# Mixture stages: GpSimd issues its row transfers to the slots in fours, each four behind a unit of the shared expert

## The chip, the core and the metric

The kernel runs on one core of a Trainium2 chip. TensorE (PE) multiplies matrices, VectorE (DVE) and ScalarE (ACT) work elementwise, GpSimd (POOL) does small elementwise work and issues the indirect DMAs, SyncE (SP) issues the plain ones. The metric is device time in microseconds, lower is better. The engines run their own instruction streams and meet at semaphores.

## What is computed

Two layers of sequence mixing and feed-forward blocks on 4096 tokens of width 256 (float32). The change concerns the last block of each half of the second layer, `_L1_ffn_ref`, which the program calls twice (stages `moe1` and `moe2`):

```python
x = x + _L1_attn_a_ref(_layernorm(x), ...)
x = x + _L1_ffn_ref(_layernorm(x), ...)      # stage moe1
x = x + _L1_attn_b_ref(_layernorm(x), ...)
x = x + _L1_ffn_ref(_layernorm(x), ...)      # stage moe2

def _L1_ffn_ref(x, gate_w, gate_bias, w_gate, w_up, w_down, sw_gate, sw_up, sw_down):
    B, N, H = x.shape
    xf = x.reshape(-1, H)
    topk_idx, topk_w = _gate(xf, gate_w, gate_bias)        # 2 of 8 experts for each token
    g = silu(einsum('th,ehi->tei', xf, w_gate))
    u = einsum('th,ehi->tei', xf, w_up)
    experts_y = einsum('tei,eih->teh', g * u, w_down)
    masked_y = take_along_axis(experts_y, topk_idx[:, :, None], axis=1)
    y = einsum('tkh,tk->th', masked_y, topk_w).reshape(B, N, H)
    shared = silu(x @ sw_gate) * (x @ sw_up) @ sw_down     # the shared expert, every token
    return y + shared
```

## The kernel before

Tokens lie in `TILES` = 32 tiles of 128, in `G` = 8 groups of four tiles. A mixture stage (`stage_moe`) normalises the tokens, transposes them for TensorE, computes the router's scores, and on VectorE chooses two experts for each token and works out a place (slot) for each of the 8192 pairs of token and choice, so that the rows of one expert stand together in DRAM (`xd`, shown in the profile as `moe_slots_moe`).

Two pieces of work then run side by side:

- **The row transfers.** GpSimd issues 64 indirect DMAs (`TOP_K` = 2 choices times 32 tiles, L2016). Each scatters the 128 rows of a tile (256 values and the token's number, 1028 bytes a row) to their slots. Before each eight of them GpSimd copies the numbers of the tokens into the rows (L2013). Each completion counts on `sent[k]`. SyncE waits for all of them (L1968) and only then loads the slots back, tile by tile (L1965), for the routed experts.
- **The shared expert.** It runs in `UNITS` = `G * SB_` = 16 units n, two for a group (blocks b = 0, 1 of the hidden width 256). TensorE's `up(n)` (L2060) multiplies gate and up weights, four products of 128x512 that the trace shows as eight matmuls; ScalarE's `silu(n)` (L2171) waits for it; VectorE's `product(n)` (L2252) multiplies and raises `prod_ready` by one. After the second unit of group g, TensorE's `down(g)` (L2069) waits for both products and writes four tiles to PSUM; it signals `y_ready` after each two of them, and VectorE adds these to `x` (`add`, L2258). The accumulators are two pairs of banks (`hp` for even n, `trp` for odd n), so `up(n)` waits for `prod_ready` at n - 1. TensorE's order is up(0), up(1), the two count products of the router, up(2), down(0), up(3), up(4), down(1) and so on. Units 0 and 1 come before the slots are known, the others beside the row transfers.

When both are done, the **routed experts** follow in 72 tiles: TensorE transposes a loaded tile (L2107), multiplies by its expert's weights (L2113, L2126), and GpSimd scatters the result to `yd` by another indirect DMA (L2020). TensorE reaches this part after down(7), whose end is also the end of the shared expert.

Nothing in the kernel before ties the row transfers to the progress of the shared expert: GpSimd issues all 64 as fast as it can from the moment that the places of the first choice are there (`idx_ready`).

Of the kernel before, what the change touches and what calls it, by code (L numbers as in the profile page):

```python
# [23 lines left out]
TILES = T // P  # L24
# [1799 lines left out]
TOP_K = 2  # L1824
# [52 lines left out]
def stage_moe(c, name, out=None):  # L1877
# [2 lines left out]
    we, ws, wsd, wr, bias, order, count, w = (m[n] for n in ("we", "ws", "wsd", "wr", "bias", "order", "count", "w"))  # L1880
    ids, starts, xd, yd, w_loaded = m["ids"], m["starts"], m["xd"][name], m["yd"], m["loaded"]
    UNITS = G * SB_
    with Local(c, name) as s:
        st = s.sb("bn_stats", [P, TILES, 6])
        mv = s.sb("moments", [P, TILES, 2])
# [45 lines left out]
        up_filled, silu_ready, prod_ready = s.sem("up_filled"), s.sem("silu_ready"), s.sem("prod_ready")  # L1931
# [15 lines left out]
        with ExitStack() as banks:  # L1947
# [13 lines left out]
            with nc.Block() as block:  # L1961
# [25 lines left out]
                @block.gpsimd  # L1987
                def _(pool):
                    pool.memset(half[:, :], -0.5).then_inc(half_ready, 1)
                    pool.memset(eps[:, :], EPS).then_inc(half_ready, 1)  # L1990
                    pool.memset(less[:, :], -1.0).then_inc(half_ready, 1)
                    pool.wait_ge(half_ready, 3)
                    for g in range(G):
                        at = slice(g * GT, (g + 1) * GT)
                        pool.wait_ge(moments_ready, g * GT + GT)
                        pool.tensor_tensor(ve[:, at], mv[:, at, 1], eps[:, :], ALU.add).then_inc(eps_added, 1)
                        pool.tensor_tensor(minus[:, at], mv[:, at, 0], less[:, :], ALU.mult).then_inc(eps_added, 1)
                        pool.wait_ge(eps_added, 2 * g + 2)
                        pool.tensor_tensor(rstd[:, at], ve[:, at], half[:, :], ALU.pow).then_inc(rstd_ready, 1)
                        pool.wait_ge(rstd_ready, g + 1)  # L2000
                        pool.tensor_tensor(shift[:, at], minus[:, at], rstd[:, at], ALU.mult).then_inc(shift_ready, 1)
                    pool.wait_ge(m["xd_padded"], 32)
                    pool.wait_ge(xn_ready, TILES // 2)
                    pool.wait_ge(xa_ready, TILES // 2)
                    pool.wait_ge(w_loaded, 16 * MOE_LOADS)
                    for choice in range(TOP_K):
                        pool.wait_ge(idx_ready, choice + 1)
                        for t in range(TILES):
                            k = t // CHUNK
                            if t % CHUNK == 0:  # L2010
                                if choice > 0:
                                    pool.wait_ge(sent[k], 16 * CHUNK)
                                pool.tensor_copy(xr[:, t:t + CHUNK, D:ROW].bitcast(U32).rearrange("p t o -> p (t o)"),  # L2013
                                                 ids[:, choice, t:t + CHUNK]).then_inc(id_ready, 1)
                                pool.wait_ge(id_ready, choice * CHUNKS_X + k + 1)
                            pool.indirect_dma_start(xd, bass.IndirectOffsetOnAxis(ap=idx[:, choice, t:t + 1], axis=0), xr[:, t, :],  # L2016
                                                    None).then_inc(sent[t // CHUNK], 16)
                    for i in range(SLOT_TILES):
                        pool.wait_ge(yt_ready, i + 1)
                        pool.indirect_dma_start(yd, bass.IndirectOffsetOnAxis(ap=xg[:, i % XRING, D:ROW].bitcast(U32), axis=0),  # L2020
                                                yb[:, i % XRING, :], None, bounds_check=TOP_K * T - 1,
                                                oob_is_err=False).then_inc(y_sent[i % XRING], 16)

                @block.tensor
                def _(pe):
# [48 lines left out]
                    def up_and_down(n):  # L2074
                        up(n)
                        if n % 2 == 0:
                            down(n // 2 - 1)
# [3 lines left out]
                    for g in range(1, G):  # L2081
# [12 lines left out]
                      .then_inc(counted, 1)  # L2094
                    for n in range(2, UNITS):
                        up_and_down(n)
                    down(G - 1)

                    pe.wait_ge(prod_ready, UNITS)
                    pe.wait_ge(added, 2 * G)  # L2100
# [60 lines left out]
                def _(act):  # L2161
# [21 lines left out]
                    def scores(n):  # L2183
                        act.wait_ge(logits_ready, n + 1)
                        for j in range(GT):
                            last = act.activation(score[:, n * STRIPS * GT:(n + 1) * STRIPS * GT, :].rearrange("p (i j) e -> p i j e", j=GT)[:, :, j, :],
                                                  back[n][:, j, :, 0:E], ACT.Sigmoid)
                        last.then_inc(score_ready, 1)
# [10 lines left out]
                    scores(1)  # L2199
                    for n in range(UNITS):  # L2200
                        silu(n)
# [23 lines left out]
                def _(dve):  # L2225
# [129 lines left out]
                    table()  # L2355
                    for n in range(2, UNITS):
                        product(n)
# [808 lines left out]
```

## Time and profile before

| | us |
|---|---|
| median of 3 runs | 3938.58 |
| lowest, highest | 3938.28, 3950.86 |
| the profiled execution's own time | 3947.42 |
| its span, first to last instruction | 3945.4 |
| PE busy in it | 3244.7 (82%) |
| DVE busy in it | 2616.1 (66%) |
| ACT busy in it | 1717.3 (44%) |
| POOL busy in it | 1533.2 (39%) |

The profiled execution lies 8.84 us above the median, within the spread of the three runs. Times within the profile are counted from the span's start; `moe1` reaches its row transfers at 2722 us, `moe2` at 3640 us. In a timeline row the columns are start, duration, engine, line, operation, what it writes and reads, how many instructions were merged, and in brackets how long the engine had been idle and what released it; "issue" there means that the profile shows nothing that it waited for, "remote" that the release was a semaphore whose sender the profile does not name.

### The profile page before, as it was taken

Reading aid. Unit: us, or ns where it says so; the run is one execution under the profiler, and the core shown is the slowest. Engines: PE = TensorE matmul, PEld = TensorE weight load, DVE = VectorE, ACT = ScalarE, POOL = GpSimd, SP = SyncE. Lnnn points to the kernel's source line nnn. Section 1 sums busy time; section 2 is a strip of 40 time slices with the busy share of each in tenths; the row PEclk is TensorE's granted clock in tenths of the full one; section 3 lists DMA queues with packets and bytes.
Section 4 is the critical chain, followed back from the end, with each engine's and each line's share of the span. In section 5 each row is a group of like instructions: output and inputs, shape, how many; then the busy total and the mean of one; then the engine's idle time right before and its main releaser. Section 6 shows DMA issues by size and latency. Waiting matters only on the chain. (4 is left out here: it accounts for less than half of the span.)

```text
span 3945.4 us, 55387 instructions
## 1 busy us (share of the span) xinstructions
PE 3244.7 (82%) x15992; PEld 1825.7 (46%) x15993; DVE 2616.1 (66%) x5017; ACT 1717.3 (44%) x3399; POOL 1533.2 (39%) x1586
## 2 busy tenths in 40 slices
PE   7898889888699698898979898776596787997495
PEld 3343334333256534434344466453374475664274
DVE  6999899999877585757668575974146673224145
ACT  5757666566355355554636553112032232222031
POOL 4898888988600212212121101534353100002533
PEclk8999999999999889798989999888798898998797
DMA  4555455565400000000000002601144792000236
GB/s 132 139 139 136 126 138 138 131 137 133 108 1 0 15 2 2 1 2 1 2 1 2 1 1 85 164 0 41 56 146 132 178 124 33 16 11 9 88 99 200
DMA packets 370273, 283.07 MB, mean 72 GB/s; under 512 B 214027, under 2 KB 290367, under 8 KB 370017
## 3 DMA queue, kind: packets, MB, share of 16 engines
q1 hardware_dynamic: 356960, 246.43, 25.5%
q0 software_dynamic: 13056, 33.65, 2.5%
q8 instruction: 110, 1.80, 0.2%
q14 instruction: 147, 1.20, 0.1%
HBM read 205.69 MB, written 76.16 MB: 71 GB/s over the span
## 5 line engine op out<-in xcount | busy, mean ns | idle before, releaser
L608 POOL TENSOR_TENSOR mamba_dBu<-mamba_du,mamba_bcs 128x512 f32<-128x512 f32 x512 | 640.3, 1272 | 127.6 <-DMA mamba_bcs<-mamba_bc 85.7
L531 PE MATMUL mamba_banks<-mamba_hc,ident 128*128 128x512 f32 x1024 | 537.8, 634 | 144.6 <-DVE mamba_hc L847 144.5
L777 ACT ACTIVATE mamba_banks<-mamba_delta,mamba_a_neg 128x512 f32<-128x512 f32 x512 | 352.3, 690 | 181.9 <-DVE mamba_hc L847 171.0
L1542 DVE TENSOR_REDUCE attn_mp<-attn_banks 128x1 f32<-128x512 f32 (+3 forms) x768 | 384.0, 551 | 69.0 <-PE attn_banks L1252 48.8
L531 PEld LDWEIGHTS mamba_banks<-mamba_hc,ident 128*128 128x128 f32 x1024 | 180.8, 195 | 459.1 <-DVE mamba_hc L847 346.6
L847 DVE TENSOR_TENSOR mamba_hc<-mamba_banks,mamba_bcs 128x512 f32<-128x512 f32 x512 | 344.3, 674 | 11.4 <-PE mamba_banks L531 11.4
L840 DVE TENSOR_TENSOR_SCAN mamba_banks<-mamba_banks,mamba_dBu 128x512 f32<-128x512 f32 x256 | 312.1, 1219 | 56.1 <-ACT mamba_banks L777 36.5
L840 DVE TENSOR_TENSOR_SCAN mamba_banks<-mamba_banks,mamba_h_end,mamba_dBu 128x512 f32<-128x512 f32 x256 | 327.3, 1279 | 20.1 <-ACT mamba_banks L777 12.2
L1249 PE MATMUL attn_banks<-attn_kT,attn_qT 96*128 96x512 bf16 (+3 forms) x768 | 272.3, 374 | 12.3 <-ACT attn_kT L1431 4.9
L1264 PE MATMUL attn_banks<-attn_qT,attn_kT 98*128 98x512 bf16 (+3 forms) x768 | 247.3, 341 | 12.5 <-ACT attn_r L1450 4.8
L939 PE MATMUL ffn_hp<-ffn_xT,ffn_w1T 128*128 128x512 f32 x512 | 231.3, 607 | 10.9 <-ACT ffn_xT L160 7.5
L2020 POOL DMA_INDIRECT moe_rows<-moe_yb,moe_xg x144 | 141.7, 984 | 219.9 <-DVE moe_yb L2374 148.7
L1450 ACT ACTIVATE attn_probs<-attn_banks 128x512 f32<-128x512 f32 (+2 forms) x256 | 111.5, 498 | 145.9 <-PE attn_banks L1264 144.4
L951 PE MATMUL ffn_yp<-ffn_w2T,ffn_hs 128*128 128x256 bf16 x1536 | 170.0, 273 | 0.0
L939 PEld LDWEIGHTS ffn_hp<-ffn_xT,ffn_w1T 128*128 128x128 f32 x512 | 97.3, 194 | 134.4 <-issue 113.0
L951 PEld LDWEIGHTS ffn_yp<-ffn_w2T,ffn_hs 128*128 128x128 bf16 x1536 | 150.3, 98 | 18.3 <-issue 0.7
L2113 PE MATMUL moe_hp<-moe_we,moe_xgT 128*128 x576 | 150.5, 384 | 0.0
L1264 PEld LDWEIGHTS attn_banks<-attn_qT,attn_kT 98*128 98x128 bf16 x768 | 73.9, 100 | 162.4 <-ACT attn_probs L1450 42.4
L2069 PE MATMUL moe_yp<-moe_wsd,moe_hs 128*128 128x256 f32 x256 | 62.3, 399 | 98.9 <-issue 96.0
L1450 ACT ACTIVATE attn_r<-attn_banks 128x512 f32<-128x512 f32 (+2 forms) x256 | 116.5, 520 | 52.9 <-PE attn_banks L1264 50.7
L2016 POOL DMA_INDIRECT moe_slots_moe<-moe_rows,moe_idx x128 | 124.3, 971 | 38.9 <-issue 37.5
L2364 DVE TENSOR_TENSOR moe_h<-moe_hp,moe_silu 128x128 f32<-128x128 f32 x144 | 42.0, 292 | 139.1 <-ACT moe_silu L2209 106.2
(389 smaller groups left out, 6665.9 us busy)
## 6 DMA issues: line engine op xcount, KB each, us to landing
mamba_bcs<-mamba_bc SPq DMA_DIRECT2D x256, 512.0 KB, 5.0
moe_slots_moe<-moe_pad SPq DMA_DIRECT2D x2, 9252.0 KB, 55.6
moe_xg<-moe_slots_moe SPq DMA_DIRECT2D x144, 128.5 KB
mix_qkv<-mixA_qkv SPq DMA_DIRECT2D x8, 1536.0 KB, 5.9
mixA_y<-moe_rows SPq DMA_DIRECT2D x16, 512.0 KB, 5.8
mix_qk<-mix_qkv SPq DMA_DIRECT2D x16, 512.0 KB, 7.7
mix_v<-mix_qkv SPq DMA_DIRECT2D x16, 256.0 KB, 7.6
mix_out<-mixB_oh SPq DMA_DIRECT2D x16, 256.0 KB, 6.9
```

Source lines behind the costliest of these rows:

```text
L531: pe.matmul(banks[:, SUMS + k % PAIR, :], c.ident[:, :], hc[:, n % RING, :], start=False, stop=True, skip_group_check=True).then_inc(sem(" ...
L608: pool.tensor_tensor(dBu[:, n % RING, :], du[:, v, k, :], bcs[:, i_of(n) % 4, 0, :], ALU.mult)\
L777: act.activation(banks[:, n % RING, :], delta[:, v, k, :], ACT.Exp, scale=a_neg[:, k, st:st + 1])\
L840: dve.tensor_tensor_scan(banks[:, n % RING, :], banks[:, n % RING, :], dBu[:, n % RING, :], 0.0 if v == 0 else h_end[:, st, k:k + 1], ALU. ...
L847: dve.tensor_tensor(hc[:, n % RING, :], banks[:, n % RING, :], bcs[:, (p * NS + st) % 4, 1, :], ALU.mult).then_inc(sem("hc_ready"), 1)
L939: mm = pe.matmul(hp[:, b % 4, :], w1T[:, k, b * P:(b + 1) * P], norm.xT[:, k, :], start=(k == 0), stop=(k == KD - 1))
L951: mm = pe.matmul(yp[:, j, :], hs[:, v, b, a, j * P:(j + 1) * P], w2T[:, b, :], start=(b == 0 and a == 0), stop=(b == HB - 1 and a == SP_ - 1))
L1249: mm = pe.matmul(banks[:, at_ring, 0:size], qT[0:KS, qt // GT, h, qt % GT * P:(qt % GT + 1) * P], kT[0:KS, h, at:at + size], start=True, s ...
L1264: pe.matmul(banks[:, SLOTS + (step * HG + j) % SLOTS, 0:size], kT[:, h, kt * P:(kt + 1) * P], qT[:, n % 2, h, at - n % 2 * 512:at - n % 2 ...
L1450: act.activation(probs[step % 3][:, j, 0:size], banks[:, SLOTS + (step * HG + j) % SLOTS, 0:size], ACT.Exp, scale=AD ** -0.5)\
L1542: dve.tensor_reduce(mp[:, qt // GT, j, qt % GT, at // 512:at // 512 + 1], banks[:, item % SLOTS, 0:size], AX.X, ALU.max).then_inc(sem("rin ...
L2113: mm = pe.matmul(gup[r % 2], xgT[:, r % 2, k * P:(k + 1) * P], we[:, :, :].rearrange("p e n -> p (e n)")[:, bass.ds(at + k * 2 * P, 2 * P) ...
```

## The change

One constant and one wait are added in `stage_moe`, so in both mixture stages:

```diff
     UNITS = G * SB_
+    PER_UNIT = TOP_K * TILES // UNITS
...
                                 pool.wait_ge(id_ready, choice * CHUNKS_X + k + 1)
+                            unit = (choice * TILES + t) // PER_UNIT
+                            if t % PER_UNIT == 0 and unit >= 2:
+                                pool.wait_ge(prod_ready, unit - 1)
                             pool.indirect_dma_start(xd, bass.IndirectOffsetOnAxis(ap=idx[:, choice, t:t + 1], axis=0), xr[:, t, :],
                                                     None).then_inc(sent[t // CHUNK], 16)
```

`PER_UNIT` is 2 * 32 // 16 = 4. The 64 transfers of a stage form 16 fours, u = 0 to 15. Before four u (u from 2 on) GpSimd waits until `prod_ready` is at least u - 1, that is until product(u - 2) of the shared expert is done. No instruction is added on another engine and none changes place. On GpSimd the built program shows it so. In `moe1`, kernel before, the fifth to seventh eight of row transfers (u = 8 to 13). The names of semaphores are those of the first stage that used the same register: `mamba_shift_ready` is `id_ready`, `mamba_z_added`, `mamba_xi_copied`, `mamba_conv_filled` and `mamba_conv_copied` belong to `idx_ready` and `sent`.

```order
L2013 COPY moe_rows<-moe_ids 128x8 [waits mamba_xi_copied,mamba_z_added]
L2016 DMA moe_slots_moe<-moe_rows,moe_idx 9216x257 [waits mamba_shift_ready]
L2016 DMA moe_slots_moe<-moe_rows,moe_idx 9216x257 x7
L2013 COPY moe_rows<-moe_ids 128x8 [waits mamba_conv_filled]
L2016 DMA moe_slots_moe<-moe_rows,moe_idx 9216x257 [waits mamba_shift_ready]
```

The same place on GpSimd in the changed kernel; `mamba_tanh_z` is `prod_ready`.

```order
L2014 COPY moe_rows<-moe_ids 128x8 [waits mamba_xi_copied,mamba_z_added]
L2020 DMA moe_slots_moe<-moe_rows,moe_idx 9216x257 [waits mamba_tanh_z,mamba_shift_ready]
L2020 DMA moe_slots_moe<-moe_rows,moe_idx 9216x257 x3
L2020 DMA moe_slots_moe<-moe_rows,moe_idx 9216x257 [waits mamba_tanh_z]
L2020 DMA moe_slots_moe<-moe_rows,moe_idx 9216x257 x3
L2014 COPY moe_rows<-moe_ids 128x8 [waits mamba_conv_filled]
```

Nothing moved: the run of eight DMAs is cut in two, and each half has the wait on `prod_ready` ahead of it. There are 14 such waits in a stage.

## Rows read from the trace of the kernel before

**Rows 1.** Timeline of moe1, PE: units of the shared expert, then the routed experts.
```profile
2738.74 3.60 PE L2060 MATMUL moe_hp<-moe_xT,moe_ws 128*128 128x512 f32 x8
2742.18 3.62 PE L2069 MATMUL moe_yp<-moe_wsd,moe_hs 128*128 128x256 f32 x16
...
2749.06 3.60 PE L2060 MATMUL moe_hp<-moe_xT,moe_ws 128*128 128x512 f32 x8
2803.88 5.86 PE L2069 MATMUL moe_yp<-moe_wsd,moe_hs 128*128 128x256 f32 x16 [51.22 <-issue]
...
2813.74 3.70 PE L2060 MATMUL moe_hp<-moe_xT,moe_ws 128*128 128x512 f32 x8 [0.57 <-DVE moe_hs L2252]
...
2850.93 0.41 PE L2107 MATMUL moe_trp<-ident,moe_xg 128*128 128x128 f32 x2 [0.83 <-issue]
```

**Rows 2.** Timeline of moe1, ACT and then DVE, beside those of PE.
```profile
2745.69 0.60 ACT L2171 ACTIVATE moe_silu<-moe_hp 128x512 f32<-128x512 f32 x1 [6.15 <-issue]
2802.50 0.60 ACT L2171 ACTIVATE moe_silu<-moe_trp 128x512 f32<-128x512 f32 x1 [56.22 <-issue]
2812.36 0.60 ACT L2171 ACTIVATE moe_silu<-moe_hp 128x512 f32<-128x512 f32 x1 [9.27 <-remote]
...
2759.10 0.69 DVE L2258 TENSOR_TENSOR x<-moe_yp,x 128x512 f32<-128x512 f32 x1 [12.10 <-remote]
2780.10 0.69 DVE L2258 TENSOR_TENSOR x<-moe_yp,x 128x512 f32<-128x512 f32 x1 [20.31 <-remote]
2803.13 0.69 DVE L2252 TENSOR_TENSOR moe_hs<-moe_trp,moe_silu 128x512 f32<-128x512 f32 x1 [22.34 <-issue]
...
2835.32 0.69 DVE L2252 TENSOR_TENSOR moe_hs<-moe_trp,moe_silu 128x512 f32<-128x512 f32 x1 [3.37 <-ACT moe_silu L2171]
```

**Rows 3.** Timeline of moe1, POOL's row transfers, and SP's first loads after them.
```profile
2722.01 1.22 POOL L2016 DMA_INDIRECT moe_slots_moe<-moe_rows,moe_idx  x1 [0.46 <-POOL moe_rows L2013]
...
2767.62 0.96 POOL L2016 DMA_INDIRECT moe_slots_moe<-moe_rows,moe_idx  x1 [0.30 <-issue]
2768.88 0.96 POOL L2016 DMA_INDIRECT moe_slots_moe<-moe_rows,moe_idx  x1 [0.30 <-issue]
...
2803.61 0.96 POOL L2016 DMA_INDIRECT moe_slots_moe<-moe_rows,moe_idx  x1 [0.30 <-issue]
...
2806.48 5.78 SPq L1965 DMA_DIRECT2D moe_xg<-moe_slots_moe  x8
```

**Rows 4.** Timeline of moe2: PE, ACT, POOL and SP in turn.
```profile
3667.38 3.60 PE L2060 MATMUL moe_hp<-moe_xT,moe_ws 128*128 128x512 f32 x8
3715.81 5.58 PE L2069 MATMUL moe_yp<-moe_wsd,moe_hs 128*128 128x256 f32 x16 [44.83 <-issue]
...
3731.95 6.03 PE L2060 MATMUL moe_hp<-moe_xT,moe_ws 128*128 128x512 f32 x8 [7.13 <-DVE moe_hs L2252]
...
3730.57 0.60 ACT L2171 ACTIVATE moe_silu<-moe_hp 128x512 f32<-128x512 f32 x1 [15.54 <-remote]
...
3640.25 1.06 POOL L2016 DMA_INDIRECT moe_slots_moe<-moe_rows,moe_idx  x1 [0.38 <-POOL moe_rows L2013]
...
3685.95 0.96 POOL L2016 DMA_INDIRECT moe_slots_moe<-moe_rows,moe_idx  x1 [0.30 <-issue]
...
3721.93 0.96 POOL L2016 DMA_INDIRECT moe_slots_moe<-moe_rows,moe_idx  x1 [0.30 <-issue]
...
3724.97 5.54 SPq L1965 DMA_DIRECT2D moe_xg<-moe_slots_moe  x8
```

**Rows 5.** Stretches of moe1: length, busy PE, PEld, DVE, ACT, POOL, clock, DMA, GB/s.
```profile
2770.00:2775.00 5.00, 0.00 (x0) 0.00 (x0) 0.00 (x0) 0.00 (x0) 3.96 (x5) 0.50 0.30 105
...
2806.60:2812.60 6.00, 6.00 (x19) 3.82 (x17) 0.00 (x0) 0.23 (x1) 0.00 (x0) 0.86 0.61 176
2812.60:2820.00 7.40, 6.83 (x23) 4.04 (x22) 3.87 (x6) 1.56 (x3) 0.00 (x0) 1.00 0.00 0
...
2860.00:2870.00 10.00, 9.45 (x52) 7.72 (x51) 4.43 (x16) 3.80 (x12) 5.42 (x6) 1.00 0.48 142
```

## The prediction

> **What bounds the kernel now.** I read the table of engines first: TensorE is busy 82% of the span, so the question for a change on GpSimd is where TensorE stands still in the two mixture stages. The list of waits for 2690 to 2860 us puts one wait of 51 us on TensorE's down product. The timeline there shows it: TensorE ends up(8) at 2752.7 and starts down(3) at 2803.88, after 51.22 us of idle time that the profile calls "issue" [rows 1]. Going back: down(3) waits for product(7), at 2803.13 on VectorE, which waits for silu(7), at 2802.50 on ScalarE [rows 2]. And silu(7) needs only up(7), which ended by the time that up(8) began, at 2749.06 [rows 1]. So TensorE's signal for up(7) took effect some 53 us late.
>
> It is not the only late one. up(6) ended at 2742.3, silu(6) ran at 2745.69: 3.4 us late. The halves of down(2) ended at about 2744 and 2745.8, and their adds ran at 2759.10 and 2780.10: 15 and 34 us late, both released by "remote". up(8) ended at 2752.7 and silu(8), whose other conditions were long met, ran at 2812.36: 60 us late [rows 1, 2]. They arrive in order, 10 to 22 us apart, while signals between ScalarE, VectorE and TensorE take hundredths of a microsecond: silu(7) ends at 2803.10 and product(7) starts at 2803.13; that ends at 2803.82 and down(3) starts at 2803.88.
>
> What else goes on: only the row transfers. [...] The late signals begin about 20 us after the first transfer. The last of them comes in at 2812.36, as the eight loads of slots behind the transfers end: DMA share 0.61 up to 2812.6, 0.00 from there on, and then TensorE runs at once at full clock [rows 2, 3, 5]. moe2 repeats it: 44.83 us idle before down(3) at 3715.81, a second stall of 7.13 us before up(10) at 3731.95, behind silu(8) at 3730.57, and SyncE's loads begun at 3724.97 [rows 4]. Together 51.2 + 44.8 + 7.1 + 0.6 = 103.7 us of the span are TensorE waiting inside dense runs of row transfers. Traffic alone does not do it: in the routed experts the DMA share is 0.48, with 142 GB/s, and TensorE is busy 9.45 of 10 us [rows 5]; there GpSimd issues less often. Why TensorE's signals come late under the transfers the trace does not say. It says that they do, and that they no longer do once the transfers have landed.
>
> **The change, part by part.** It adds 14 waits a stage on GpSimd. Behind each are queued the other row transfers, and behind the last of these SyncE's wait for all of them and the loads for the routed experts.
>
> *Where the wait does not bind.* Undisturbed, TensorE takes 10.32 us for two units (up(6) at 2738.74, up(8) at 2749.06) [rows 1], 5.16 us for one. Four transfers cost GpSimd the same: four 0.96 with gaps of 0.30, and a token copy each eight. When the run begins, two products are already there and a third follows at once, so GpSimd has slack. Fours 0 to 8 find their products (the last, product(6), comes at about 2747) and go out as before, up to the DMA of 2767.62, which ends at 2768.58 [rows 3]. So the first stall begins as before, and cannot be avoided by this change. A wait that is met costs a few hundredths of a microsecond; at the outside the 0.3 us gap of a transfer, 4 us in a stage, on GpSimd and off the path.
>
> *Where it binds.* Four 9, in the kernel before at 2768.88, needs product(7), which is the late one. GpSimd stops. The transfers drain: in the kernel before it took 2806.48 - 2804.57 = 1.9 us from the last to SyncE's first load [rows 3]. If the signals get through then, silu(7) starts at 2768.58 + 1.9 = 2770.5, and down(3), 1.38 us after silu(7) as before (2802.50 to 2803.88), at 2771.9. Gain 2803.88 - 2771.9 = 32.0 us; the 0.57 us before up(10) [rows 1] goes too, as silu(8) no longer comes late: 32.6 us.
>
> In moe2 the ninth four ends with the DMA of 3685.95, at 3686.91, drained at 3689.0 (3724.97 - 3722.89 = 2.1 us) [rows 4]; down(3) at 3690.4, 25.4 us earlier. Behind it the 7.13 us stall goes, and up(10), 6.03 us long after that stall for the usual 3.60 [rows 1, 4], is 2.4 us shorter: 34.9 us. Both stages: **67.5 us**.
>
> *What it may give back.* After the restart 28 transfers are left, now in step with the units and with almost no slack. Their mean pace, one each 1.29 us or slower, is hardly slower than 1.26. In the first run signals came late after some 18 transfers (2722.01 to 2745.69) [rows 2, 3], so I expect the stall to come back once, near the 17th of the 28. But now GpSimd is at most one four ahead and stops at its next wait. At worst that is a whole four, 5.1 us, 1.9 us to drain, 1.4 us to the next product, and a product at the lower clock (5.86 for 3.62 us [rows 1]) 2.2 us: 10.6 us. The least is nothing. I take the middle, 6 us a stage, 12 in all; as no row shows a restart, 0 and twice 10.6 a stage (two relapses) are the bounds.
>
> *Is something else late next?* The routed experts start after down(7) and after the first load. down(7) moves from 2850.9 to 2818.3. product(13), on which the last four waits, moves from 2835.32 to 2802.7 [rows 2]; the four is out by about 2808.5, landed at 2810.4, and the first eight loads had moved their data 6 us after that moment in the kernel before (2806.5 to 2812.6) [rows 3, 5]. That is 2816.4 for all eight, 2 us of cover, and the first tile needs only the first of them. A relapse shifts both alike. So nothing is added, but the 44 us that lay between last transfer and first routed tile shrink to about 10.
>
> Gain 67.5 - 12 = 55.5 us. Against the profiled execution: 3947.4 - 55.5 = 3891.9. That execution lies 8.8 us above the median of the runs shown, and the stalls are no reason for that, so the forecast for the median is 3938.6 - 55.5 = **3883 us**.
>
> **The rivals.**
>
> *The stall is paid once and does not return.* The stopped engines may be waiting for something of their own that stands behind the row transfers in the DMA engines, and once it has come the second half runs free. For it: ScalarE's wait before silu(7) is called "issue", and it makes no difference to the first gain. Against: two neighbouring adds on VectorE each waited on their own, 12.10 and 20.31 us [rows 2], and both stages stall at the same unit though their code lies elsewhere. Gain 67.5 us, 3871.
> [...]
>
> *The stall comes back again and again.* With pace 1.29 against 1.26 us the fours keep TensorE's signals late as soon as they run, and draining takes 8 us, as after the last transfer of both stages (2804.57 to 2812.36), not 2. Then 6 us are lost on the first gain and twice 8 on the rest of each stage: 67.5 - 2 x 22 = 23.5, 3915.
>
> *Pausing GpSimd does not free the signals.* If the late signals take their time whatever GpSimd does, product(7) comes at 2803.8 as before, and GpSimd has stood since 2768.6. Then 28 transfers are still to be issued beside the second half, which in the kernel before ran almost free of them. They take 36 us, to 2840, and a second stall begins after some 20 us of them: 16 us to their end and up to 8 more for draining, with 1.4 to restart, less what TensorE has in hand (3.6 us): about 21 us a stage. 3938.6 + 42 = 3981, slower. It decides by whether silu(7) follows the pause or keeps its 2802. Against it: the delays ended with the traffic in both stages.
>
> *The waits never bind*, because TensorE's products are early enough. Then nothing changes, 3939. The trace speaks against it: product(7) comes 35 us after four 9 could have gone.
>
> **How the numbers follow.** Forecast (one short relapse a stage) 0.43; paid once, 3871, 0.25; repeated relapses, 3915, 0.15; no effect 0.05; slower, 3981, 0.12. The range has to hold 8 in 10: it takes in the first three, from 3871 less the 9 us that runs of this kernel differ by, 3862, to 3915 plus 10 for the worst of the relapses, 3925. About 0.3% (12 us) is what a measurement of this kernel can tell from no change; all of the first three lie beyond it. Faster 0.83, same 0.05, slower 0.12.
>
> **What would show it.** In the timeline of moe1 GpSimd stops after its 36th row transfer, at about 2768.6, for a few microseconds and is released by product(7). silu(7) at 2770 to 2772 proves the main step; at 2802 refutes it. The idle time before down(3) falls from 51.2 to about 19 us in moe1 and from 44.8 to about 19 in moe2. A second gap of 3 to 10 us on TensorE at units 12 to 14 is the relapse; none is the first rival. The first routed transposes begin at 2820 to 2826, with no wait for a load. The forecast is wrong if the stall ends otherwise than with the traffic, or if it begins sooner when transfers and products run in step.

## The result, and the profile after

| | before | changed |
|---|---|---|
| median, us | 3940.56 (4 runs) | 3887.26 (4 runs) |
| lowest, highest | 3938.28, 3950.86 | 3883.0, 3888.13 |
| profiled execution, its span | 3947.42, 3945.4 | 3887.37, 3885.7 |
| mean granted clock | 0.917 | 0.925 |

The ratio is 0.9857, with an interval of 0.9843 to 0.987: 1.4% faster, 4 us from the forecast of 3883. The span is 59.7 us shorter. All of it is in the two mixture stages: from a stage's first row transfer to its first routed transpose it was 128.9 us in `moe1` and 131.2 in `moe2` (2722.01 to 2850.93 in [rows 1, 3]), and is 100.0 and 100.3: 28.9 + 30.9 = 59.8 us.

The timeline of `moe1`, changed kernel, PE. `down` is now L2073, `up` L2064, the routed transpose L2111. These rows answer to [rows 1].

```profile
2747.97 3.60 PE L2064 MATMUL moe_hp<-moe_xT,moe_ws 128*128 128x512 f32 x8
2773.22 5.26 PE L2073 MATMUL moe_yp<-moe_wsd,moe_hs 128*128 128x256 f32 x16 [21.66 <-DVE moe_hs L2256]
...
2797.44 3.72 PE L2073 MATMUL moe_yp<-moe_wsd,moe_hs 128*128 128x256 f32 x16 [1.77 <-DVE moe_hs L2256]
...
2816.33 3.72 PE L2073 MATMUL moe_yp<-moe_wsd,moe_hs 128*128 128x256 f32 x16 [1.41 <-DVE moe_hs L2256]
2820.88 0.41 PE L2111 MATMUL moe_trp<-ident,moe_xg 128*128 128x128 f32 x2 [0.83 <-issue]
```

The idle time before down(3) fell from 51.22 to 21.66 us. A second, small stall stands before down(5): 1.77 us. The 1.41 us before down(7) are no stall: down(7) follows up(15) at once and has to wait for its product; runs without late signals show the same 1.41. ScalarE's silu(7) and silu(11), of the same stage, then the row transfers on POOL and the first loads on SP's queue, which answer to [rows 2, 3]:

```profile
2771.84 0.60 ACT L2175 ACTIVATE moe_silu<-moe_trp 128x512 f32<-128x512 f32 x1 [29.97 <-remote]
...
2796.07 0.60 ACT L2175 ACTIVATE moe_silu<-moe_trp 128x512 f32<-128x512 f32 x1 [10.08 <-PE moe_hp L2064]
```
```profile
2766.54 0.96 POOL L2020 DMA_INDIRECT moe_slots_moe<-moe_rows,moe_idx  x1 [0.30 <-issue]
2773.44 0.96 POOL L2020 DMA_INDIRECT moe_slots_moe<-moe_rows,moe_idx  x1 [5.94 <-DVE moe_hs L2256]
...
2797.66 0.96 POOL L2020 DMA_INDIRECT moe_slots_moe<-moe_rows,moe_idx  x1 [3.89 <-DVE moe_hs L2256]
...
2811.78 0.96 POOL L2020 DMA_INDIRECT moe_slots_moe<-moe_rows,moe_idx  x1 [0.30 <-issue]
...
2814.37 3.66 SPq L1966 DMA_DIRECT2D moe_xg<-moe_slots_moe  x8
```

GpSimd's 36th transfer ends at 2767.50. It then stands for 5.94 us and is released by product(7). silu(7) got its signal at 2771.84, 4.3 us after that end; in the kernel before it got it at 2802.50 [rows 2]. At the 53rd transfer GpSimd stands again, 3.89 us, because silu(11) came 3.8 us late. The last transfer ends at 2812.74, and the loads follow 1.63 us later.

`moe2`, changed kernel: PE, ACT, POOL in turn; they answer to [rows 4].

```profile
3662.98 5.81 PE L2073 MATMUL moe_yp<-moe_wsd,moe_hs 128*128 128x256 f32 x16 [20.80 <-DVE moe_hs L2256]
...
3698.64 3.72 PE L2073 MATMUL moe_yp<-moe_wsd,moe_hs 128*128 128x256 f32 x16 [2.34 <-DVE moe_hs L2256]
...
3661.60 0.60 ACT L2175 ACTIVATE moe_silu<-moe_trp 128x512 f32<-128x512 f32 x1 [29.11 <-remote]
...
3663.20 0.96 POOL L2020 DMA_INDIRECT moe_slots_moe<-moe_rows,moe_idx  x1 [5.09 <-DVE moe_hs L2256]
```

In the table of stretches the pause looks so (length, busy PE, PEld, DVE, ACT, POOL, clock, DMA share, GB/s), against 0.30 and 105 GB/s in [rows 5]:

```profile
2767.50:2772.50 5.00, 0.00 (x0) 0.00 (x0) 0.03 (x1) 0.66 (x2) 0.00 (x0) 0.50 0.07 26
```

### The profile page after: what moved, and what is told of

It is laid out like the page before. It is cut to its first block and busy times, and to the rows that moved or that the text cites. A ratio compares the mean times of both kernels' runs of the same rounds, so it can differ in the third digit from the quotient of the medians.

```text
span 3885.7 us, 55401 instructions
## 1 busy us (share of the span) xinstructions
PE 3238.9 (83%) x15992; PEld 1820.9 (47%) x15993; DVE 2615.3 (67%) x5017; ACT 1717.6 (44%) x3399; POOL 1535.8 (40%) x1586
## 5 line engine op out<-in xcount | busy, mean ns | idle before, releaser
L608 POOL TENSOR_TENSOR mamba_dBu<-mamba_du,mamba_bcs 128x512 f32<-128x512 f32 x512 | 640.0, 1271 | 128.9 <-DMA mamba_bcs<-mamba_bc 83.1
L840 DVE TENSOR_TENSOR_SCAN mamba_banks<-mamba_banks,mamba_dBu 128x512 f32<-128x512 f32 x256 | 312.1, 1219 | 59.7 <-ACT mamba_banks L777 35.7
L1403 POOL TENSOR_SCALAR_AFFINE_SELECT attn_stk<-attn_stk 128x512 f32<-128x512 f32 x48 | 30.5, 636 | 256.2 <-ACT attn_stk L1450 256.2
```

Of the source, the lines that this page charges most:

```text
L608: pool.tensor_tensor(dBu[:, n % RING, :], du[:, v, k, :], bcs[:, i_of(n) % 4, 0, :], ALU.mult)\
L840: dve.tensor_tensor_scan(banks[:, n % RING, :], banks[:, n % RING, :], dBu[:, n % RING, :], 0.0 if v == 0 else h_end[:, st, k:k + 1], ALU. ...
```

## The experiments

The theory: TensorE's signals come late because row transfers follow each other densely, and they get through when GpSimd pauses. Its rivals: a single event such as a code fetch behind the transfers; the bytes moved rather than the number of transfers; and, within the theory, whether the pace, the landing of what is out, or the tie to TensorE's progress does the work. All kernels but the tied ones start from the kernel before, without the change's waits. Times below are counted from the stage's first row transfer, `moe1` then `moe2`. "Pace" is the mean distance of the 64 transfers, 1.295 us in the kernel before. The lateness of a step of ScalarE or VectorE is counted from the end of the TensorE product that it waits for; where nothing disturbs it, silu starts 0.04 us after that end, and under 1.5 us is not called late. After the occasion of the result above, the runs fell on four more, each with one chip and its own runs of the kernel before: the first four kernels, the next four (rest before each second, rest twice, tie one step closer, rest before each again), three more, and the last one. Only times are kept of the kernel before on these four; its one trace is the one behind [rows 1] to [rows 5].

**Wait for landings.** Before each eight, GpSimd waits until the eight before has landed.

```diff
                             if t % CHUNK == 0:
                                 if choice > 0:
                                     pool.wait_ge(sent[k], 16 * CHUNK)
+                                if choice > 0 or k > 0:
+                                    pool.wait_ge(sent[(k - 1) % CHUNKS_X], 16 * CHUNK * (choice + (k > 0)))
```

> The kernel before, with no tie to the products; instead GpSimd waits, before each eight row transfers, until the eight before have landed (seven short pauses in a stage). Theory A (dense row transfers pile something up that delays TensorE's signals after some 18 of them, and it empties when they have landed): no late signal at all, idle time before down(3) under 1 us in both stages instead of 51 and 45. The eights then take 10.3 + 2 us each, GpSimd ends near 2722 + 98 = 2820, and the routed experts wait for it and start near 2824 instead of 2851: about 3940 - 54 = 3886 us. Theory B (each engine waits for something of its own, such as code, that stands behind the transfers): the stall stays at the same unit, down(3), and ends at one of the pauses, 8 to 20 us long. Theory C (what helps is only that GpSimd stands while TensorE catches up, so a pause of 2 us does too little): idle time before down(3) 40 us or more, 3930 to 3950 us.

3889.0 us beside 3946.83, one run of each. The pace was 1.53 us, and no signal came late in either stage. Its timeline of `moe1`, POOL, then PE:

```profile
2743.81 0.20 POOL L2015 COPY moe_rows<-moe_ids 128x8 uint32<-128x8 uint32 x1 [1.78 <-DMA moe_slots_moe<-moe_rows,moe_idx]
...
2788.24 3.72 PE L2071 MATMUL moe_yp<-moe_wsd,moe_hs 128*128 128x256 f32 x16 [1.41 <-DVE moe_hs L2254]
...
2820.04 0.66 PE L2109 MATMUL moe_trp<-ident,moe_xg 128*128 128x128 f32 x2 [28.09 <-DMA moe_xg<-moe_slots_moe]
```

GpSimd pauses 1.7 to 3.0 us ahead of each eight. down(7) runs 70 us after the first transfer, and the 28.09 us idle behind it are a wait for the loads: the transfers, now ending at 97.6, have become the bound. The routed part starts at 101.7 and 100.8, hardly another time than with the change. So short pauses suffice to prevent the stall, without any tie to TensorE. Whether by the landing or by the pace, this run does not tell.

**A slower pace alone.** One small memset on GpSimd, and a wait for it, ahead of each transfer.

```diff
+                            pool.memset(rest_a[:, :], 0.0).then_inc(rested, 1)
+                            pool.wait_ge(rested, choice * TILES + t + 1)
                             pool.indirect_dma_start(xd, ...
```

> The kernel before, with one tiny memset and a wait for it ahead of each row transfer, so that they go out one each 1.7 us or so instead of 1.26; no pause, no tie to the products. If the pace is what counts (the routed experts bear one indirect DMA each 1.63 us without a late signal): no stall, GpSimd ends near 2722 + 64 x 1.7 = 2831 and the routed experts start near 2837, 14 us earlier than before: about 3912 us. If the number since the last pause is what counts: late signals from the 18th transfer, at 2753, to the end near 2833, and then still 46 us of shared expert: 30 us a stage slower than before, about 4000 us. If it is a matter of code: stall at down(3) as before, ended by nothing in particular.

3871.5 us beside 3946.83 (one run each), at a pace of 1.40 us. ScalarE and PE, `moe1`:

```profile
2767.41 0.60 ACT L2174 ACTIVATE moe_silu<-moe_trp 128x512 f32<-128x512 f32 x1 [8.50 <-remote]
...
2783.74 6.65 PE L2072 MATMUL moe_yp<-moe_wsd,moe_hs 128*128 128x256 f32 x16 [4.37 <-DVE moe_hs L2255]
...
2807.09 5.23 PE L2072 MATMUL moe_yp<-moe_wsd,moe_hs 128*128 128x256 f32 x16 [13.27 <-issue]
```

The late signals are still there, but they begin at 50 us on ScalarE instead of 23.7 (2745.69 - 2722.01 [rows 2, 3]), and cost 18 us of idle time a stage, not 52. 0.11 us more between transfers does this, with nothing awaited. The same kernel timed in more runs, on another occasion:

> The kernel before with one small memset and a wait for it ahead of each row transfer, mean pace 1.40 us, as seen once at 3871.5 us; now timed. If that look was typical: 3871 +- 4 us, ratio to the kernel before 0.982, below the changed kernel's 0.9857. If the late stall near the end is chancy: spread over 10 us.

3895.4 us median (3886.42 to 3909.39, 4 runs), ratio 0.988, interval 0.9855 to 0.9905. The spread of 23 us, against 5 for the changed kernel, says that this pace lies at the edge. In the profiled run, the fastest of the four, ScalarE's first late step comes at 40.5 us already, and PE stood 7.25 + 17.02 us in `moe1`. So the single run of 3871.5 us was not typical, as its repetition had expected it to be (3871 +- 4).

**Half the bytes.** Of each row 129 of 257 values are transferred, to a narrower table in DRAM, at the same pace. The first 128 values of each token are zero for the routed experts, so part of the computation is left out; the engines' work is the same, and SyncE's loads behind the transfers are halved too.

```diff
-                            pool.indirect_dma_start(xd, ..., xr[:, t, :],
+                            pool.indirect_dma_start(xd2, ..., xr[:, t, P:ROW],
```

> The kernel before, where each row transfer carries the last 129 of a row's 257 values only, into and out of a narrower table of slots; the first 128 columns that the routed experts read are zero, so the output is not the reference's. As many transfers and rows as before, at the same pace, half the bytes (516 for 1028 a row). If bytes in the DMA engines are what piles up: no late signal, idle before down(3) 0, and the routed experts start at the floor, near 2808 to 2812: gain about 40 us a stage, 3860. If it is the issuing of transfers or their descriptors: stall as before, 51 and 45 us, about 3938. Between them, a stall that begins later, at twice as many transfers, 36: gain about 20 a stage, 3900.

3937.62 us beside 3946.83 (one run each). The stretch of `moe1` that lies in the transfers, and PE in `moe2`:

```profile
2740.00:2790.00 50.00, 18.27 (x48) 10.47 (x46) 2.08 (x3) 0.60 (x1) 38.22 (x43) 0.70 0.16 52
```
```profile
3693.14 6.29 PE L2075 MATMUL moe_yp<-moe_wsd,moe_hs 128*128 128x256 f32 x16 [26.38 <-issue]
...
3715.55 5.33 PE L2066 MATMUL moe_hp<-moe_xT,moe_ws 128*128 128x512 f32 x8 [12.67 <-issue]
3728.07 5.90 PE L2075 MATMUL moe_yp<-moe_wsd,moe_hs 128*128 128x256 f32 x16 [7.19 <-DVE moe_hs L2259]
```

52 GB/s for 105, a DMA share of 0.16 for 0.30, and 26.4 + 12.7 + 7.2 = 46.3 us of stall in each stage; the routed part starts at 127.9 and 128.0, nearly as before. Half of the bytes left some nine tenths of the stall of `moe1` (46.3 us for 51.8), though in three parts, with silu(7) in at 55.7 us and not at 80.5. So it is not mainly a matter of bytes; the number of transfers in time remains.

**One pause for landing.** GpSimd waits once, ahead of four 9, where the change first binds, until all 36 transfers have landed, and then goes on as before.

```diff
+                            if choice == 1 and t == 4:
+                                pool.wait_ge(sent[CHUNKS_X - 1], 16 * CHUNK)
+                                pool.wait_ge(sent[0], 16 * (CHUNK + 4))
                             pool.indirect_dma_start(xd, ...
```

> The kernel before, with one pause a stage: ahead of four 9 (after 36 transfers) GpSimd waits only until the 36 have landed, some 2 us, not for a product. Theory A: the late signals come in during that pause or shortly after it, silu(7) at 2770 to 2773 and down(3) 31 us earlier; the other 28 transfers run densely, and after some 18 of them, near 2794, signals are late again until the end at 2807: a second gap of 8 to 14 us on TensorE. About 19 us gain a stage, 3902. Theory B: no second gap, 3873. Theory C (only a real stop for TensorE helps): silu(7) stays late, at 2790 or later, over 3920.

3940.8 us beside 3946.83 (one run each), where the theory had expected about 3902. ScalarE, POOL and PE, `moe1`:

```profile
2772.80 0.60 ACT L2174 ACTIVATE moe_silu<-moe_trp 128x512 f32<-128x512 f32 x1 [29.91 <-remote]
2779.82 0.60 ACT L2174 ACTIVATE moe_silu<-moe_hp 128x512 f32<-128x512 f32 x1 [6.42 <-issue]
2812.14 0.60 ACT L2174 ACTIVATE moe_silu<-moe_trp 128x512 f32<-128x512 f32 x1 [31.73 <-remote]
```
```profile
2770.96 0.96 POOL L2019 DMA_INDIRECT moe_slots_moe<-moe_rows,moe_idx  x1 [2.38 <-issue]
```
```profile
2774.17 5.30 PE L2072 MATMUL moe_yp<-moe_wsd,moe_hs 128*128 128x256 f32 x16 [21.61 <-issue]
...
2813.52 6.11 PE L2072 MATMUL moe_yp<-moe_wsd,moe_hs 128*128 128x256 f32 x16 [27.18 <-DVE moe_hs L2255]
```

This is the run that shows what the change's waits do. A pause of 2.38 us lets silu(7) in at 50.9 us, just as in the changed kernel, so the pause ends the first stall. But GpSimd goes on before that, and silu(8) gets its signal only 6.4 us after silu(7)'s end, at 57.9; down(4) then stands 27.18 us, for an expected 8 to 14. The 2.38 us were enough for one signal and gave no lasting relief: the routed part starts at 127.8 and 127.7, nearly as in the kernel before. Two things are different with the change. Its pause lasts until the product is there, twice as long or more (5.94 and 5.09 us), and silu(8) runs within it, at 51.4 us, before GpSimd goes on at 52.5. And afterwards GpSimd goes at TensorE's pace (from the 37th transfer to the 64th 1.42 us each, here 1.29) and stops whenever a product is late. Which of the two gains more no run shows.

**The pace once more, from both sides.** A memset and wait before every second transfer (pace 1.376 us), and two before each (1.559 us).

```diff
+                            for _ in range(1 if t % 2 == 1 else 0):      # the other kernel: range(2)
+                                rests += 1
+                                pool.memset(rest_a[:, :], 0.0).then_inc(rested, 1)
+                                pool.wait_ge(rested, rests)
                             pool.indirect_dma_start(xd, ...
```

> The kernel before with one small memset and a wait for it ahead of every second row transfer, no tie to products. Up to here, signals of TensorE were late from 20.5 us after the first transfer at a mean pace of 1.295 us, from some 34 us at 1.403, and never at 1.534. Theory R (a reservoir: one transfer is worked off each 1.61 us, an estimate from the first two of these, and about 3 may be outstanding before signals are late): at a mean pace of 1.35 the first late signal comes after 3.08 / (1/1.35 - 0.622) = 26 us, some 19 transfers. Theory N (it is the count since the last rest, 16, and a rest of 0.1 us does not reset it): at 21.6 us. Theory S (any short gap between transfers is enough to let a signal through): no late signal. The time lies between before and the kernel with a rest at each transfer (3871.5): 3885 to 3920.

> The kernel before with two small memsets and waits ahead of each row transfer, mean pace about 1.51 us, no pauses for landing and no tie. Theory R: 3.08 / (1/1.51 - 0.622) = 77 us before the first late signal, when TensorE has almost finished the shared expert: no stall over 2 us; GpSimd ends 96 us after its first transfer and the routed experts start at 102 us, later than the 96 of one rest and the 100 of the changed kernel: about 3889 us. Theory L (what cured the stall in the kernel with landings awaited each eight is the landing, not the pace): a stall comes here in spite of the pace, at 40 us or so, with 20 us or more of idle TensorE before one of its products.

3945.27 and 3893.59 us, one run of each, beside 3944.66 (3943.25 to 3954.05, 7 runs). PE in `moe1` of the first, then of the second:

```profile
2762.36 5.54 PE L2075 MATMUL moe_yp<-moe_wsd,moe_hs 128*128 128x256 f32 x16 [10.77 <-issue]
...
2813.03 5.79 PE L2075 MATMUL moe_yp<-moe_wsd,moe_hs 128*128 128x256 f32 x16 [31.30 <-DVE moe_hs L2258]
```
```profile
2823.27 0.66 PE L2113 MATMUL moe_trp<-ident,moe_xg 128*128 128x128 f32 x2 [29.56 <-DMA moe_xg<-moe_slots_moe]
```

At 1.376 us silu(7) is ScalarE's first late step, at 40.1 us, and in `moe2` at 35.9 us, 8.6 late; the stall is only shifted: PE stands 47 and 45 us, nothing is won. VectorE's adds are late sooner: the first at 25.3 us in `moe1`, 3.1 late, near the 26 us that the reservoir had been expected to give, which at 1.403 us is 44.5, and 37.6 in the repetition. At 1.559 us none is late; the loads bind, as with the landing waits, and the routed part starts at 103.0. At about the same pace, then, resting does what waiting for landings did. So far:

| pace, us | ScalarE's first late step in moe1: when, how late | idle of PE for it, moe1 |
|---|---|---|
| 1.295 (before) | 23.7, by 3.4 | 51.8 |
| 1.376 | 40.1, by 12.8 | 47.1 |
| 1.403 | 50.2, by 2.2 | 17.6 |
| 1.403, repeated | 40.5, by 2.9 | 25.1 |
| 1.533 (landing awaited) | none | 0 |
| 1.559 | none | 0 |

**The tie one step closer.** The changed kernel with four u waiting for product(u) instead of product(u - 2).

```diff
-                            if t % PER_UNIT == 0 and unit >= 2:
-                                pool.wait_ge(prod_ready, unit - 1)
+                            if t % PER_UNIT == 0:
+                                pool.wait_ge(prod_ready, min(unit + 1, 14))
```

> The changed kernel with a tighter tie: four u waits for product(u) instead of product(u - 2), the last ones for product(13). GpSimd has less to spare when the first late signal comes, 20 us after its start, and stops at four 6 or 7 instead of 9, some 10 to 12 us earlier. Theory (the first stall lasts until GpSimd stops and 4 us more): idle time before down(3) falls from 21 to about 10 us, the rest in step as in the changed kernel, routed experts at 94 to 98 us after the first transfer instead of 100: 3876 us, ratio to the kernel before 0.983. Rival (a tighter tie makes GpSimd wait for TensorE all the time and the last transfers late): 3890 or more.

3882.78 us median (3873.34 to 3887.3, 4 runs), ratio 0.9833, interval 0.9811 to 0.9855, which overlaps the change's 0.9843 to 0.987: no difference between the two is shown. GpSimd first stands after 28 transfers, behind product(7) too, and `down(3)` waits 10.64 us instead of 21.66:

```profile
2764.34 0.96 POOL L2020 DMA_INDIRECT moe_slots_moe<-moe_rows,moe_idx  x1 [5.18 <-DVE moe_hs L2256]
...
2764.12 5.60 PE L2073 MATMUL moe_yp<-moe_wsd,moe_hs 128*128 128x256 f32 x16 [10.64 <-DVE moe_hs L2256]
```

11 us won at the first stall; later small ones (1.62 and 4.01 us, and 1.96 for a load) take part of it back, and the routed part starts at 95.7 and 95.6 instead of 100.

**Three that met no stall.** The next runs were made to tell landing from pace (the landing awaited before each sixteen), to use one stage as the control of the other (the change's waits in `moe1` alone), and to join the rests with the tie.

```diff
+                                if (choice > 0 or k > 0) and k % 2 == 0:
+                                    pool.wait_ge(sent[(k - 1) % CHUNKS_X], 16 * CHUNK * (choice + (k > 0)))
```
```diff
-                            if t % PER_UNIT == 0 and unit >= 2:
+                            if t % PER_UNIT == 0 and unit >= 2 and out is None:
```
```diff
+                            if t % 4 == 0:
+                                pool.wait_ge(prod_ready, min((choice * TILES + t) // 4 + 1, 14))
+                            rests += 1
+                            pool.memset(rest_a[:, :], 0.0).then_inc(rested, 1)
+                            pool.wait_ge(rested, rests)
```

> The kernel before, where GpSimd waits before each sixteen row transfers (three times a stage) until the sixteen before have landed, some 2 us each; dense at 1.295 us within a sixteen, mean pace about 1.39. It parts the two ways in which awaiting landings each eight may have helped there. If landing empties what had piled up: each sixteen ends at 20.7 us, just where signals began to be late (20.5 us), so no signal is late by more than 2 us, TensorE does not stall, GpSimd ends at 82.6 + 6 = 89 us after its first transfer, the routed experts start at 94 to 95 us: about 3872 us. If only the mean pace counts and the reservoir is not emptied by a pause: late signals from 35 to 45 us on, a stall of 10 to 50 us, routed experts at 96 to 128 us: 3880 to 3940 us.

> The change in moe1 alone; in moe2 GpSimd issues as before. If the two stages are independent and each gives half: 28.9 us of the 59.7 us of span in moe1, so 29 us less than the kernel before, ratio 0.9926; idle before down(3) 21 us in moe1 and 45 us in moe2. If the gain in one is partly given back later in the other: less than 25 us.

> Both cures together: a small memset and wait ahead of each row transfer (mean pace 1.40 us) and four u tied to product(u), the last to product(13). With 1.40 us signals get late only after 35 to 45 us, and then GpSimd stops at once, being never more than one four ahead. If that holds: stalls of TensorE of 3 us at most at a time, GpSimd ends at 90 to 92 us, routed experts at 95 to 98 us in every run, without the spread that the rest alone had: 3876 us, ratio 0.983. If the tie costs GpSimd more than the stall cost TensorE: routed experts at 100 us or more, 3885 us.

On this occasion the kernel before itself took 3863.46 us (3858.73 to 3870.14, 16 runs), 77 us less than where the change was measured, so there can hardly have been a stall in it to be told apart. Waits in `moe1` alone: 3864.39 us, ratio 1.000 (0.9989 to 1.001). Its trace has a stage with the change and one without. In the table of stretches, the 83 us from the first transfer on, `moe1` with the waits and `moe2` without, which issues as the kernel before does:

```profile
2715.89:2798.70 82.81, 71.81 (x228) 42.71 (x226) 25.57 (x48) 7.76 (x13) 63.75 (x71) 0.96 0.29 101
3593.16:3676.00 82.84, 71.84 (x228) 42.73 (x226) 25.62 (x49) 7.76 (x13) 63.79 (x71) 0.96 0.29 101
```

And the same 83 us of `moe1` in the kernel before, where it stalled:

```profile
2722.01:2804.57 82.56, 30.97 (x94) 17.59 (x93) 13.11 (x30) 2.98 (x5) 63.54 (x71) 0.71 0.29 101
```

GpSimd does the same in all three (63.5 to 63.8 us busy, 71 instructions), and the DMA engines too (0.29, 101 GB/s). TensorE is busy 71.8 us in two of them and 30.97 in the third. So neither the code nor the traffic alone decides it; something that differs between the occasions does, and no run shows what. The kernels with landings awaited before each sixteen (3877.25 us, one run) and with rests and tie (3874.88 us, ratio 1.0026, interval 1.0014 to 1.0037) say only what holding the transfers back costs where nothing stalls: the loads bind, the routed part starts at 92 to 94 us, not at 86.7. Landing against pace stayed open.

**The change once more.** The changed kernel itself, unedited, on the fourth occasion.

> The changed kernel once more beside the kernel before, on whatever chip comes. In the last three runs the kernel before took 3863 us and TensorE did not stall in either stage, with or without the waits, where on three occasions before it took 3941 to 3947 and stalled. If the chip (or what goes on around it) decides whether signals come late: either a kernel before of 3939 to 3947 us with a ratio of 0.984 to 0.987 and the stall of 21 us in the changed one, or a kernel before near 3863 us with a ratio within 0.003 of 1 and routed experts at 87 to 89 us after the first transfer, no wait of GpSimd for a product over 1 us. If the late signals are chance in each run, whatever the chip: times of the kernel before spread between the two levels within this one set.

3863.84 us (3856.55 to 3875.08, 10 runs) beside 3864.21 (3857.5 to 3871.05, 13 runs): ratio 1.0003, interval 0.9992 to 1.0014. The chip has the same number as the one of the first occasion, where the kernel before took 3946.83; whether it is the same chip is not known. There is no stall in the changed kernel's trace, none of the 28 waits held GpSimd for over 1 us, and the time of the kernel before leaves no room for one. PE in its `moe1`:

```profile
2808.33 0.66 PE L2111 MATMUL moe_trp<-ident,moe_xg 128*128 128x128 f32 x2 [13.07 <-DMA moe_xg<-moe_slots_moe]
```

The whole gain of the change exists where TensorE's signals come late; where they don't, none is measured.

## What the traces of the two kinds of occasion show besides

**No packet of the instruction queues ends the stall.** The rival with a fetch of code can be put to the trace. The page's list of DMA queues has two of the kind "instruction", with 110 and 147 packets in the whole span of the kernel before; that they carry code is taken from their kind alone. Over 3662 to 3732 us, the whole stall before down(3) of `moe2` in the kernel before [rows 4], the list of queues (packets, MB, share of 16 engines) has these lines and no more:

```profile
q0 software_dynamic: 2313, 6.32, 25.6%
q1 hardware_dynamic: 1152, 1.05, 5.4%
```

Had ScalarE waited for a packet of these queues that stood behind row transfers, that packet would have moved just ahead of silu(7), at about 3714. None moved in these 70 us, nor in `moe1` from 2788 to 2813. One packet of 8 KB did move in the stall of `moe1`, at about 2775, and it released nothing: the next late step, VectorE's add, came at 2780.10 and silu(7) at 2802.50. And the run that rested twice ran the same code for ScalarE with no late step.

**Records of completions are missing where signals are late.** Each of the 64 row transfers of a stage counts its completion in 16 steps, 1024 in all, and the trace records such steps. Counted in `moe1`, where the third column is PE's idle time there for late signals:

| kernel | steps recorded, of 1024 | idle of PE, us |
|---|---|---|
| before, and half the bytes | 183, 217 | 51.8, 46.3 |
| one pause for landing | 219 | 48.8 |
| rest before each second | 225 | 47.1 |
| changed | 302 | 23.4 |
| rest before each, repeated | 307 | 25.1 |
| tie one step closer | 315 | 16.3 |
| rest before each | 356 | 17.6 |
| landing awaited before each eight | 641 | 0 |
| rest twice | 957 | 0 |
| the four kernels of the third and fourth occasion | 1024 | 0 |

In the list of DMA issues this shows as a missing number. The changed kernel in `moe1`, 2725 to 2742 us, where it gained, and then on the fourth occasion; the last figure is the time from issue to landing:

```profile
moe_slots_moe<-moe_rows,moe_idx POOLq DMA_INDIRECT x13
```
```profile
moe_slots_moe<-moe_rows,moe_idx POOLq DMA_INDIRECT x14, 2.6
```

The order of the table is almost the order of the stalls. But missing records are no sign of a stall by themselves. In the routed experts of `moe1`, the trace of the kernel before has 444 of 1152 steps of the loads and 549 of 1152 of the scatters, that of the changed kernel on the fourth occasion 1144 and 1151, and from first to last transpose the part took 125.2 and 125.4 us. So the loss goes with the occasion in the first place, and within it with the density of the transfers. Lost records and late signals may be two sides of one thing, a path for semaphore events that is slow on the first occasions and not on the later ones. That is an inference, and no run tests it. It fits that the number of transfers counted and not their bytes, since the steps are the same for a short row. It also raises a doubt: every run listed here carries a span and a granted clock, so each was recorded, and no run shows whether the stall is there when nothing is recorded. The recording may be part of its cause.

## Why the prediction was right, and where it was off

- *What bounds the kernel.* Right for the occasion that the trace was from: 103.7 us of TensorE waiting. That this belongs to the kernel was an assumption that I did not see as one. The median of the kernel before is 3864 on other occasions.
- *Where the wait does not bind.* Right. The first 36 transfers went out undisturbed, with the same gaps of 0.28 and 0.30 us ahead of fours 2 to 8 as in the kernel before, so a wait that is met cost nothing that shows; and the first late signals came all the same, if less late: the halves of down(2) 6.4 and 18.0 us for 15 and 34, silu(6) on time.
- *Where it binds.* Four 9, released by product(7), as said. The drain was mis-sized: silu(7) came 4.3 and 3.5 us after GpSimd's last transfer ended, not 1.9 and 2.1. It had been taken from SyncE's wait for the last transfer. But that is another signal; TensorE's late ones were on their way still, and in the kernel before they had needed until 2812.36, 7.8 us after the end. The idle before down(3) was 21.7 and 20.8 us for "about 19".
- *What it gives back.* One short relapse a stage, as said. In `moe1` GpSimd's pause came 16 transfers after the restart, for "near the 17th". In `moe2` a pause of 1.45 us came there too, but the one that goes with TensorE's idle time, 3.53 us ahead of the 61st transfer, came after 24. The price was too high: 1.8 and 2.3 us of idle time for 6, less even than the 3 to 10 us named as the sign. The clock was not lost: down(5) in `moe1` and down(6) in `moe2` took 3.72 us, not 5.86, at a granted clock of 1.00. And the pace of 1.29 us was compared with 1.26, the distance within an eight; the mean before was 1.295, so the tie by itself slows nothing down, and 1.44 came out by its pauses. The two errors, 3.8 us too little for the drains and 7.9 too much for the relapses, leave 4.1 us, about what the measured gain of span (59.7 us) has over the forecast (55.5); that the forecast came so close owes something to luck.
- *Late next.* Right: routed transposes at 2820.88, no wait for a load. The 44 us between last transfer and first routed tile shrank to 8.1 (2812.74 to 2820.88).
- *Paid once and not returning.* Refuted where the stall exists, by the one pause for landing, after which it came back (48.8 us of idle time in all for 51.8), and by the instruction queues: the page counts 110 and 147 packets on them, but in `moe1` of the kernel before the one in the stall moved at about 2775, 5 us ahead of the late add at 2780.10, and in `moe2` none moved from 3662 to 3732.
- *Again and again.* This is what a pause without a tie does, 27.18 us before down(4). With the tie it stays at single microseconds.
- *Pausing GpSimd does not free the signals.* Refuted in both stages.
- *The waits never bind* had 0.05. On the last occasion it is what happened, 3864 for both kernels, and on the one before it for the waits in `moe1` alone. The chance was too low, since one trace of one occasion says nothing on how the next will be.

One caution belongs to all readings of "up(7) ended". The end that the timeline shows for it lies 53.3 us ahead of silu(7) in `moe1` of the kernel before and 23.7 us ahead in the changed one, and where no signal is late a silu starts 0.04 us after the end shown. Whether the data or only the signal was late the rows can't show.

## What to carry to other kernels

Where an engine waits under "remote" or "issue" although its producer ended long before, look for another engine's dense run of small DMAs, and see how many completions the trace fails to record, which here marked the occasions with stalls. Tying each few of them to the consumer's progress cost nothing measurable where there was no stall (ratio 1.0003) and gained 1.4% where there was. Unconditional rests or landing waits prevent the stall as well, but only at a pace (1.53 us here) at which the transfers become the bound, and rests joined with a tie cost 0.3% where none threatens. Run the kernel before beside the changed one on more than one occasion before a gain of this kind is called the kernel's.

## What the runs showed of the hardware, unexpected

- The same kernel ran at 3941 to 3947 us on some occasions and at 3863 to 3864 on others, and within an occasion all its runs lie in 14 us, none at the other level. The 76 to 83 us between them are mostly the stalls: 103.7 us of waiting less 2 x 13.1 us in which TensorE, no longer stalled, waits for the first load, 77.5 us.
- A distance of 1.40 us between row transfers instead of 1.295 took 34 us off the stall of `moe1` on one occasion and 27 on another, and 1.376 on that other only 5. Between these two paces the gain is steep.
- In a stall TensorE's granted clock was at 0.50 (2770 to 2775 us of the kernel before, 2767.5 to 2772.5 of the changed one). The first product after idle times of 4 us or more took 5.2 to 6.7 us for 3.6, the one after 1.4 to 2.3 us took 3.7.
